# One-core language-model block with routed experts: shorter register loads, up weights copied by VectorE for more steps, four results sent before the last scatter

## What is computed

```
h = tok(x)                                   # 8 x 512 x 192
h = h + attention(layernorm(h))              # one head, per batch
g = layernorm(h) @ Wg                        # 8 experts
top 2 experts of each token, softmax of the 2 scores
h = h + sum over the 2 of share * (gelu(layernorm(h) @ W1[e] + b1[e]) @ W2[e] + b2[e])
```

## Time and profile before

| | us |
|---|---|
| median of 3 runs | 309.22 |
| lowest, highest | 307.13, 311.77 |
| the profiled execution | 310.88 |
| its span in the profile | 308.8 |

### The profile page before, as it was taken

How to read it: one execution, slowest core, us unless ns; L and a number is a source line. 1 busy time by engine, 2 the same in 40 slices (tenths; PEclk the granted TensorE clock), 3 DMA queues, 4 the chain that set the end, 5 groups by cost and what they waited for, 6 DMA issues and landing times.

```text
span 308.8 us, 6215 instructions
## 1 busy us (share of the span) xinstructions
PE 224.5 (73%) x1552; PEld 152.9 (50%) x1552; DVE 170.1 (55%) x675; ACT 121.5 (39%) x292; POOL 209.5 (68%) x281
## 2 busy tenths in 40 slices
PE   0750892487855889778785966988999999899800
PEld 0540651233423335344544755866778787777600
DVE  5745999747999896748877461000223221474522
ACT  1002021426622313456244462455666655545400
POOL 5776885812997887777667757777665765777540
PEclk9999998555875555589555699699999999999975
DMA  7810006990000000000011111332222223898735
GB/s 175 253 16 12 1 7 233 361 344 20 0 2 0 10 12 11 13 17 15 15 41 41 43 38 45 108 108 92 81 79 81 67 83 82 314 315 277 259 84 192
DMA packets 25822, 30.47 MB, mean 99 GB/s; under 512 B 15290, under 2 KB 19249, under 8 KB 25595
## 3 DMA queue, kind: packets, MB, share of 16 engines
q1 hardware_dynamic: 19308, 22.13, 23.1%
q0 software_dynamic: 6480, 7.94, 8.3%
HBM read 14.72 MB, written 16.02 MB: 100 GB/s over the span
## 4 chain that ended last, share of the span: by engine, by line
PE 35%; DVE 18%; SPq 14%; issue 11%; DMA 8%; POOL 7%; ACT 5%; DVEq 0%; POOLq 0%; ACTq 0%
PE bank_b L2063 16%; POOL circuit L511 5%; DMA shares_out<-circuit,up 4%; PE bank_a L1828 4%; SPq L456 4%; SPq L450 4%; PE bank_b L1821 4%; SPq L457 3%; PE bank_a L2051 3%; SPq L452 3%; PE bank_c L1840 2%; DVE nmax L1168 2%; DMA angle_stages<-shares_out 2%; PE bank_d L1779 1%; POOL rs L683 1%
## 5 line engine op out<-in xcount | busy, mean ns | idle before, releaser
L745 POOL DMA_INDIRECT shares_out<-circuit,up x71 | 72.8, 1025 | 33.4 <-issue 15.8
L2063 PE MATMUL bank_b<-wide,up 128*128 x426 | 90.4, 356 | 6.3 <-ACT up L1686 2.4
L2063 PEld LDWEIGHTS bank_b<-wide,up 128*128 128x128 f32 x426 | 71.4, 199 | 21.9 <-issue 21.8
L694 POOL DMA_INDIRECT routed<-rows,slot x64 | 62.0, 968 | 25.3 <-issue 19.2
L1508 DVE COPY up<-wide 32x384 f32 x47 | 18.2, 387 | 66.6 <-PE bank_a L2051 50.0
L1698 ACT ACTIVATE circuit<-bank_b,up 128x192 f32<-128x192 f32 x71 | 29.9, 422 | 40.5 <-PE bank_b L2063 39.0
L511 POOL DMA_INDIRECT circuit<-angles,ids x32 | 31.3, 978 | 10.8 <-issue 9.0
L1686 ACT ACTIVATE up<-bank_a 128x384 f32<-128x384 f32 x71 | 34.5, 489 | 6.5 <-PE bank_a L2051 6.5
L1828 PE MATMUL bank_a<-keys_t,wt 32*128 32x512 f32 x64 | 27.6, 949 | 3.8 <-DVE nmax L1168 2.1
L1821 PE MATMUL bank_b<-queries_t,keys_t 32*128 32x512 f32 x64 | 26.1, 900 | 5.7 <-ACT keys_t L1537 2.5
L1168 DVE TENSOR_REDUCE nmax<-bank_a 128x2 f32<-128x1024 f32 x16 | 19.5, 1220 | 11.2 <-PE bank_a L1828 11.2
(11 more groups left out here) (430 smaller groups left out, 380.0 us busy)
## 6 DMA issues: line engine op xcount, KB each, us to landing
routed<-pad_rows SPq DMA_DIRECT2D x8, 528.0 KB, 5.2
out<-hres SPq DMA_DIRECT2D x8, 384.0 KB, 3.3
wide<-down_w SPq DMA_DIRECT2D x1, 2304.0 KB, 12.9
prob<-shares_out SPq DMA_DIRECT2D x3, 768.0 KB
angle_stages<-shares_out SPq DMA_DIRECT2D x3, 768.0 KB
up<-up_w SPq DMA_DIRECT2D x1, 1536.0 KB
form_p<-shares_out SPq DMA_DIRECT2D x2, 768.0 KB, 6.7
up<-routed SPq DMA_DIRECT2D x71, 16.0 KB, 1.7
```

Of the source, the lines that this page charges most:

```text
L694: pool.indirect_dma_start(out=routed, out_offset=bass.IndirectOffsetOnAxis(slot[:, b, k, j:j + 1], 0), in_=rows[:, b, k, j, :], in_offset=None
L745: pool.indirect_dma_start(out=shares_out, out_offset=bass.IndirectOffsetOnAxis(xb[:, m, DEST:DEST + 1].bitcast(I32), 0), in_=y[:, m % RESU ...
L2063: mm = pe.matmul(bank_b[:, m % 2, 0:D], hid[:, m % STEP, c * P:(c + 1) * P], wide_flat[:, bass.ds(first + c * D, D)], start=(c == 0), stop ...
```

## The change

1. Each register load goes through `register`, which states the bounds of the value without the instructions that test them at run time. This holds on SP, PE and DVE.
2. Only steps 0 to 2 have their up weights loaded by SP (`LOADED_STEPS = 3`). DVE copies those of steps 3 to 17, into a ring of eight tiles instead of two.
3. On DVE all eight `add_experts` stand behind all copies.
4. `landed` and its waits on POOL are gone. ACT waits for the semaphore of the buffer that it overwrites; SP waits for all 24 buffer semaphores (`all_added`).
5. On SP the first three `load_sums` stand together, each `store(b)` of batches 0 to 3 ahead of `load_sums(b + 3)`, and the stores of 4 to 6 ahead of the last `load_sums`.
6. On POOL the results of blocks 0 to 3 stand between `scatter(7, 0)` and `scatter(7, 1)`.

```
-    LAG = 4
-    ADDS_FROM = (2 * HALF * SEQ // P + E) // STEP + 4
+    LOADED_STEPS = 3
+    UP_TILES = 8
+    AHEAD = 4
...
-        up_now = behind(up_room, "p (r h) -> p r h", r=2, h=HID)
+        up_now = [behind(up_room, "p (h) -> p h", h=HID) for r in range(2)]
...
-        up_early = [behind(up_room_1 if s < 4 else expert_room, "p (h) -> p h", h=HID) for s in range(EARLY_STEPS)]
+        up_now += [behind(up_room_1 if r < 6 else expert_room, "p (h) -> p h", h=HID) for r in range(2, UP_TILES)]
...
+        def register(eng, entry, most):
+            return eng.value_load(entry).with_bounds(min_val=0, max_val=most)
+
+        def all_added(eng, count):
+            for n in range(RESULTS):
+                eng.wait_ge(added[n], 16 * len(range(n, count, RESULTS)))
...
             for s in range(EARLY_STEPS):
                 for m in blocks_of(s):
                     load_block(m)
-                for m in blocks_of(s):
-                    load_up(m)
+                if s < LOADED_STEPS:
+                    for m in blocks_of(s):
+                        load_up(m)
...
-            for b in range(BATCHES):
-                sp.wait_ge(landed, blocks_until(b))
+            all_added(sp, blocks_until(0))
+            for b in range(SUMS):
                 load_sums(b)
-                if b > 0:
-                    store(b - 1)
+            for b in range(SUMS, BATCHES - 1):
+                store(b - SUMS)
+                if blocks_until(b) > blocks_until(b - 1):
+                    all_added(sp, blocks_until(b))
+                load_sums(b)
+            for b in range(BATCHES - 1 - SUMS, BATCHES - 1):
+                store(b)
+            all_added(sp, BLOCKS)
+            load_sums(BATCHES - 1)
             store(BATCHES - 1)
...
+                if b == BATCHES - 1:
+                    for m in range(AHEAD):
+                        result(m)
                 scatter(b, 1)
...
-            for m in range(BLOCKS):
-                pool.wait_ge(y_done, m + 1)
-                if m >= LAG:
-                    all_landed(m - LAG)
-                pool.indirect_dma_start(
...
+            for m in range(AHEAD, BLOCKS):
+                result(m)
...
             def expert_up(s):
-                if s >= EARLY_STEPS + 2:
-                    dve.wait_ge(hid_done, s - 1)
+                if s >= UP_TILES:
+                    dve.wait_ge(hid_done, s - UP_TILES + 1)
...
-            for s in range(EARLY_STEPS, STEPS):
+            dve.wait_ge(early_done, 1)
+            for s in range(LOADED_STEPS, STEPS):
                 expert_up(s)
-                if s >= ADDS_FROM:
-                    add_experts(s - ADDS_FROM)
-            for b in range(STEPS - ADDS_FROM, BATCHES):
+            for b in range(BATCHES):
                 add_experts(b)
...
                 if m >= RESULTS:
-                    act.wait_ge(landed, m - RESULTS + 1)
+                    act.wait_ge(added[m % RESULTS], 16 * (m // RESULTS))
...
             def first_of(m):
-                return pe.value_load(table_of(m)[m:m + 1, 1:2], min_val=0, max_val=(E - 1) * WIDE)
+                return register(pe, table_of(m)[m:m + 1, 1:2], (E - 1) * WIDE)
```

More of the change, by code:

```diff
@@ L354, in build @@
         up_out = sem("up_out")
-        early_up_in = [sem(f"early_up_in{s}") for s in range(EARLY_STEPS)]
+        early_up_in = [sem(f"early_up_in{s}") for s in range(LOADED_STEPS)]
         block_in = [sem(f"block_in{s}") for s in range(STEPS)]
@@ L363, in build @@
         added = [sem(f"added{n}") for n in range(RESULTS)]
-        landed = sem("landed")
         up_ready = sem("up_ready")
@@ L449, in load_up @@
             def load_up(m):
-                row = sp.value_load(t_early[m:m + 1, 2:3], min_val=0, max_val=(E - 1) * F)
+                row = register(sp, t_early[m:m + 1, 2:3], (E - 1) * F)
                 n = m % STEP
-                sp.dma_start(up_early[m // STEP][n * F:(n + 1) * F, :], up_rows[bass.ds(row, F), :]
+                sp.dma_start(up_now[m // STEP][n * F:(n + 1) * F, :], up_rows[bass.ds(row, F), :]
                              ).then_inc(early_up_in[m // STEP], 16)
             def load_block(m):
-                row = sp.value_load(table_of(m)[m:m + 1, 0:1], min_val=0, max_val=ROWS - P)
+                row = register(sp, table_of(m)[m:m + 1, 0:1], ROWS - P)
                 sp.dma_start(xb[:, m, :], routed[bass.ds(row, P), :]).then_inc(block_in[m // STEP], 16)
@@ L697, in scatter, with result @@
                         ).then_inc(scattered_early if b < HALF else scattered_late, 16)
+            def result(m):
+                pool.wait_ge(y_done, m + 1)
+                pool.indirect_dma_start(
+                    out=shares_out, out_offset=bass.IndirectOffsetOnAxis(xb[:, m, DEST:DEST + 1].bitcast(I32), 0),
+                    in_=y[:, m % RESULTS, :], in_offset=None, bounds_check=2 * TOKENS - 1,
+                    oob_is_err=False).then_inc(added[m % RESULTS], 16)
             def constants():
@@ L734, in _ @@
                     rstd2(b + 1)
+                if b == BATCHES - 1:
+                    for m in range(AHEAD):
+                        result(m)
                 scatter(b, 1)
-            def all_landed(m):
-                pool.wait_ge(added[m % RESULTS], 16 * (m // RESULTS + 1))
-                pool.sem_inc(landed, 1)
-            for m in range(BLOCKS):
-                pool.wait_ge(y_done, m + 1)
-                if m >= LAG:
-                    all_landed(m - LAG)
-                pool.indirect_dma_start(
[L746 to L750, removed]
+            for m in range(AHEAD, BLOCKS):
+                result(m)
         @block.vector
@@ L1502, in expert_up @@
             def expert_up(s):
[L1503 to L1504 removed]
+                if s >= UP_TILES:
+                    dve.wait_ge(hid_done, s - UP_TILES + 1)
                 for n, m in enumerate(blocks_of(s)):
                     r = slice(n * F, (n + 1) * F)
[L1507 to L1508 removed]
+                    first = register(dve, table_of(m)[m:m + 1, 1:2], (E - 1) * WIDE)
+                    copied = dve.tensor_copy(up_now[s % UP_TILES][r, :], wide_flat[r, bass.ds(first + HC * D, HID)])
                 copied.then_inc(up_ready, 1)
             dve.wait_ge(table_done, 1)
[L1512 removed]
+            dve.wait_ge(early_done, 1)
+            for s in range(LOADED_STEPS, STEPS):
                 expert_up(s)
[L1514 to L1516 removed]
+            for b in range(BATCHES):
                 add_experts(b)
@@ L2033, in up_proj @@
             def up_proj(s):
-                if s < EARLY_STEPS:
-                    weights = up_early[s]
+                weights = up_now[s % UP_TILES]
+                if s < LOADED_STEPS:
                     pe.wait_ge(early_up_in[s], 16 * STEP)
                 else:
-                    weights = up_now[:, s % 2, :]
-                    pe.wait_ge(up_ready, s - EARLY_STEPS + 1)
+                    pe.wait_ge(up_ready, s - LOADED_STEPS + 1)
                 pe.wait_ge(xt_copied, s + 1)
```

## The result

The changed kernel took 299.21 us in the median of 4 runs (298.97 to 299.53), the kernel before 310.07 us (307.13 to 311.77, 4 runs). The ratio is 0.9681, with a 95% interval of 0.9606 to 0.9756; one run of the kernel before (311.77) was in a slower state, and the ratio compares the means of the others, so it is not the quotient of the two medians. The forecast was 297.4 us, with a range of 293.0 to 303.5. The profiled span fell from 308.8 to 297.3 us, where 297.0 (308.8 - 11.8) was expected.

A forecast was written before the change was run, and what follows sets the result against it. SP's loads, then PE, were taken to bound the kernel; after the change POOL would, its last result starting 11.8 us earlier with the tail kept: 309.22 - 11.8 = 297.4 us, range 293.0 to 303.5.

The forecast's parts named there:

- POOL becomes the bound: POOL's scatters and results, 1.292 us per result, set the end: last result starts at 284.7 us, 11.8 us earlier.
- rival C: VectorE's copies block POOL for 0.35 us each; twelve cost 4.2 us, giving 301.6 or 303.1 us; chance 0.10.
- SP's loads: SP's early loads: 36 at 0.95 us take 34 instead of 55 us; PE's four waits, 4.9 us, go.
- PE's clock: PE after step 3's wait: without the idleness ahead of the clock drop, 0.8 us saved, a quarter of 3.4.
- PE's queue: PE per block: two instructions, 0.17 us, go; half of 8.0 us taken, 4 us; last product at 282.8 us.
- Rival A: PE's gap between blocks is not the bounds test's; PE ends at 286.8 us, time 300.4 us; chance 0.18.
- The cover of the moved dispatch: Step 6 on PE: rows come at 203.4 us, PE reaches the transpose at 205.4, cover 2.0 us.
- rival B: The late dispatch makes PE idle at step 6 and its clock fall; gain 6.4 us, time 302.8 us; chance 0.12.
- The four moved results: Four results on POOL ahead of the last scatter fill no gap, so alone they are worth 0.
- The removed waits: POOL's waits on landings: their worth lies inside the 11.8 us; bounds alone 0 and 3.2 us.
- Rival D: Unlimited results meet the 768 KB loads; 32 results take 1.95 us each instead of 1.292; time 318 us; chance 0.05.
- The tail: After the last result: load of the last batch's results, additions and store stay at 9.9 us.

The follow-up runs named there:

- e4: The changed kernel with AHEAD = 0, the four results behind the whole dispatch again; 296.97 us, ratio 0.9568 to the kernel before.
- e3: The changed kernel with the bounds test put back into DVE's register loads alone; 296.24 us, ratio 0.9524 to the kernel before.
- e7: The changed kernel with LOADED_STEPS = 6, SP loading the up weights of steps 3 to 5 again; 296.98 us, ratio 0.9555 to the kernel before.
- e5: The kernel before with only the lighter register loads, on SP, PE and DVE; 304.76 us, ratio 0.9817 to the kernel before.
- e2: The changed kernel with the bounds test put back into PE's register loads alone; 300.86 us, ratio 0.9656 to the kernel before.
- e1: The changed kernel run once more, unaltered, as a yardstick on the first chip; 298.49 us, ratio 0.9581 to the kernel before.
- e12: The changed kernel run a third time, unaltered, as a yardstick on the third chip; 298.50 us, ratio 0.9634 to the kernel before.
- e8: The changed kernel with POOL's wait for the landing of result m - 4 put back ahead of result m; 308.24 us, ratio 0.9894 to the kernel before.
- e10: The kernel before with only POOL's waits on landings removed, SP and ACT waiting on buffer semaphores; 310.28 us, ratio 1.0012 to the kernel before.

## Why the prediction was right, and where it was not

**POOL becomes the bound: right.** No pause from 180.2 us on, and the last result starts at 284.45 (forecast 284.7). e4 shows it from the other side: PE 7 us faster, no change in the interval. The close agreement is partly luck, since terms missed and cancelled. From `scatter(7, 0)` to the last result I had 284.7 - 181.7 = 103.0 us, and it took 104.3; but this stretch began 1.5 us earlier than before, at 180.20, which no step had. Within it, DVE's additions lengthened POOL's transfers by 1.6 us in sum (spans of 1.06 to 1.24 instead of 0.99, ahead of the last), not 2.4. And the copies, priced at 0 from eight transfers beside spaced copies, lengthened 14 transfers to 1.04 to 1.14 us, 1.7 us in sum, or 2.1 with the three that stand beside later copies (103.0 + 2.1 - 0.8 = 104.3); spaced out as in e3 they cost 0.9. That is rival C's mechanism at half of its price, and with 44 copies, not the twelve that C counted. What I missed is that the same edit which lightens DVE's loads brings the copies from 0.76 to 0.47 us apart, and that the ring of eight tiles lets 44 follow one another, so the rows of before did not show the case.

**SP's loads: right.** 0.90 us each (0.95 assumed), and the four waits of the earlier trace rows went. I did not ask whether the weights had to move for it: e7 and e5 show that the light loads alone do it.

**PE's clock: right in kind, a third of its size.** It stayed at 1.00 from 178 to 201 us without the wait in step 3. I took 0.8 us for it, a quarter of 3.4. e2 has the same register loads on PE as the kernel before and a clock of 1.00 there: from `up_proj` of step 3 to that of step 4 it takes 192.38 - 185.38 = 7.00 us, the kernel before, with a mean clock of 0.64, 199.66 - 190.19 = 9.47. The drop had cost 2.5 us.

**PE's queue: right in kind, halved for no good reason.** A step without residual pieces takes 5.17 instead of 5.85 us: 0.17 per block, the whole of the two instructions. I took half and expected the last product at 282.8; it came at 278.5. Behind step 6's transpose PE saved 6.2 us (80.9 to 74.7 from there to the last product), not 4: less than 47 x 0.17 = 8.0, and there its clock had fallen once more. The other 2.1 us of the miss lie ahead of step 6. ACT did not hold PE up much in the steady part (two waits of 0.8 and 0.9 us from 222 to 278). Rival A is out, by the weight loads of both kernels and by e2.

**The cover of the moved dispatch: wrong.** I gave 2.0 us and PE waited 3.10. The rows of step 6 came as computed (PE's transpose at 203.75, forecast 203.4), but PE was there at 200.65, not 205.4. My sum took the wait of 0.45 us off twice (212.09 - 6.2 is 205.9), had too little for the clock (0.8 for 2.5), let the shorter blocks begin only with block 24 (from `up_proj` of step 3 to that of step 5, e2 takes 13.93 us and e1, with the shorter blocks, 12.80), and PE began 1.3 us earlier (178.90 for 180.17 in step 2). The wait is not a steady figure either: the same kernel waited 2.84 us in e1 and 1.69 in e12. It did no harm, since POOL was behind PE by then. So rival B's mechanism was there, without its price. The four moved results themselves were worth 0, as forecast.

**The removed waits: the term that was mis-sized.** I gave them 0 to 3.2 us of the 11.8. e8 measured 9.7 and e10 about nothing. I had priced them in a kernel where PE set the pace. Once POOL has no slack, each landing above 5.2 us stops it, and such landings come where the 768 KB loads run. In the changed kernel, the first of these lines is for 180 to 240 us and the second for 240 to 297 (count, median us to landing):

```profile
shares_out<-circuit,up POOLq DMA_INDIRECT x37, 2.4
...
shares_out<-circuit,up POOLq DMA_INDIRECT x34, 4.8
```

Without this part the change would have ended at 308.2 us (e8), a case that none of my rivals had. Rival D is out: landings were that slow, and POOL dispatched every 1.29 us all the same.

**The tail: nearly.** Load, additions and store took 297.3 - 287.64 = 9.7 us (forecast 9.9). From the last result's start to that load it was 3.2 us instead of 2.4.

**The sum.** 11.8 us forecast; 11.5 in the spans, 10.9 between the medians. Against the 309.22 us that the forecast started from, 299.21 is 10.0 us less, so the 297.4 was 1.8 us too low.

## What to carry to other kernels

When an edit makes the bound engine faster, price every other edit anew on the engine that is bound next: a wait that costs nothing behind a slower partner can cost 10 us there, and one that costs 10 us can be cured by a longer lag instead of its removal. In a busy matrix engine read the weight loads and the queue, not the matrix instructions: two small register instructions per block of 1.17 us were 15% of it here. Ask what a faster loop does to its neighbours; here slower register loads on VectorE were the faster choice.

## What the runs showed of the hardware

Indirect transfers issued by GpSimd took 0.96 to 0.99 us of the engine in most places, mostly 1.10 beside VectorE copies of 32x384 float32 that stood 0.47 us apart, and mostly 0.96 to 1.01, with seven of 1.05 to 1.14 up to 221 us, beside the same copies 0.76 apart (e3). The Trainium skill ("SBUF — State Buffer", section "SBUF: two separate sides") says that while VectorE copies float32 from SBUF to SBUF, GpSimd is locked out of the port pair that they share and cannot write the descriptors of its transfers. The runs show a price, but of 0.12 us in the mean for each of the 14 transfers, beside some three copies of 0.35 us each.

The landing of an indirect transfer of one block doubled in the median, from 2.4 to 4.8 us, while loads of 768 KB and stores of 384 KB ran (changed kernel, up to and behind 240 us), and reached 7.8 us. It did not slow the engine that issued them: POOL stood 0.30 us between transfers all the while.
